# Attention scores as pairs of 64-row products instead of a block diagonal of keys, in a fused two-layer transformer kernel

## The reference, cut to what matters

```python
x = L0_attn_x                                  # (8, 512, 128)
xn = _layernorm(x, axis=-1)
k = _layernorm((xn @ Wk).reshape(b, t, 16, 8), kln_w, kln_b)
q = _layernorm((xn @ Wq).reshape(b, t, 16, 8), qln_w, qln_b)
v = (xn @ Wv).reshape(b, t, 16, 8)
dot = einsum('bqhs,bkhs->bhqk', q, k) / sqrt(8)
dot = where(causal, dot, -inf)
attn = softmax(dot, axis=-1)
out = einsum('bhqk,bkhs->bqhs', attn, v).reshape(b, t, 128) @ Wo + bo
```

## Time and profile before

| | before |
|---|---|
| median of 3 runs | 1091.5 us (1090.92 to 1092.26) |
| profiled execution, first to last instruction | 1086.1 us |
| difference, which lies outside the profiled span | 5.4 us |
| attention stage (first q unit to last pv item) | 243.1 to 629 us of the span |
| PE, ACT, DVE, POOL busy over the whole span | 919.8, 625.7, 712.3, 569.8 us |

### The profile page before, as it was taken

The page is one execution under the profiler, slowest core; times in us unless marked ns, Lnnn a source line. Parts: engine busy times, 40 slices in busy tenths (PEclk is TensorE's granted clock), DMA queues, the critical chain, the costliest instruction groups (busy, mean ns, idle before and its releaser), DMA issues.

```text
span 1086.1 us, 20632 instructions
## 1 busy us (share of the span) xinstructions
PE 919.8 (85%) x6577; PEld 615.8 (57%) x6614; DVE 712.3 (66%) x1512; ACT 625.7 (58%) x1129; POOL 569.8 (52%) x645
## 2 busy tenths in 40 slices
PE   7688879988999899899999868677788886999980
PEld 4366654477555555555555446454555655998870
DVE  6788852125777677677766565999857673646374
ACT  6466664421887687678778746344478664333320
POOL 3400019261675566656642217999306771888772
PEclk9899989999999999999999969879989998999995
DMA  5011111434010010100101049900011102223277
GB/s 144 1 78 78 77 79 58 135 128 135 21 31 21 22 30 21 31 21 21 30 21 30 2 79 149 298 11 0 1 39 43 51 28 79 83 78 92 73 204 219
DMA packets 83841, 74.46 MB, mean 69 GB/s; under 512 B 6786, under 2 KB 76876, under 8 KB 81712
## 3 DMA queue, kind: packets, MB, share of 16 engines
q1 hardware_dynamic: 73392, 64.03, 22.3%
q0 software_dynamic: 4608, 6.64, 1.9%
q10 hardware_dynamic: 5760, 2.70, 0.9%
HBM read 34.14 MB, written 33.70 MB: 62 GB/s over the span
## 4 chain that ended last, share of the span: by engine, by line
PE 32%; DVE 18%; POOL 10%; issue 9%; ACT 2%; DMA 1%; ACTq 0%; DVEq 0%; POOLq 0%
PE banks L2030 6%; PE banks L2002 5%; PE banks L2016 5%; POOL y_dram L975 4%; PE banks L2056 3%; DVE B_mneg L1150 2%; PE banks L2004 2%; DVE D_dmx L1282 2%; PE banks L2114 2%; PE banks L2069 2%; PE banks L2165 1%; DVE banks L1331 1%; DVE D_sc L1308 1%; POOL x L951 1%; DVE D_pr L1293 1%
## 5 line engine op out<-in xcount | busy, mean ns | idle before, releaser
L1150 DVE TENSOR_REDUCE B_mneg<-banks 128x2 f32<-128x256 f32 (+3 forms) x256 | 208.5, 824 | 76.9 <-PE banks L2004 68.3
L1669 ACT ACTIVATE B_pt<-banks 128x1024 f32<-128x1024 f32 (+3 forms) x256 | 178.7, 708 | 72.9 <-PE banks L2016 67.8
L792 POOL TENSOR_SCALAR_AFFINE_SELECT B_pt<-B_pt 128x512 f32<-128x512 f32 x128 | 81.2, 634 | 170.4 <-ACT B_pt L1669 161.3
L2002 PE MATMUL banks<-B_kp,B_qt 128*128 128x128 bf16 (+3 forms) x507 | 124.7, 299 | 1.8 <-DVE B_mneg L1150 0.6
L2016 PE MATMUL banks<-B_qt,B_kp 128*128 128x256 bf16 (+3 forms) x480 | 105.2, 297 | 12.1 <-issue 5.2
L2004 PE MATMUL banks<-B_mask_q,B_identb 128*128 128x128 bf16 x512 | 101.8, 219 | 0.7 <-issue 0.6
L2030 PE MATMUL banks<-B_pt,B_vp 128*32 128x512 f32 (+3 forms) x1024 | 95.5, 445 | 1.4 <-ACT B_ot L1675 0.7
L1819 ACT ACTIVATE F_gh<-banks 128x512 f32<-128x512 f32 (+1 forms) x96 | 50.0, 526 | 78.8 <-PE banks L2234 74.2
L930 POOL DMA_INDIRECT rows_dram<-F_xs,F_rowi x64 | 62.4, 975 | 60.2 <-issue 59.6
L2165 PE MATMUL banks<-D_qk 128*128 128x512 f32 x128 | 74.9, 671 | 10.2 <-DVE D_pr L1293 10.2
L975 POOL DMA_INDIRECT y_dram<-F_yo,F_ide x60 | 60.8, 1014 | 37.8 <-DVE F_yo L1510 17.4
(11 more groups left out here) (292 smaller groups left out, 2192.3 us busy)
## 6 DMA issues: line engine op xcount, KB each, us to landing
comb_dram<-C_comb SPq DMA_DIRECT2D x8, 1024.0 KB, 3.9
C_cst<-comb_dram SPq DMA_DIRECT2D x8, 1024.0 KB, 4.8
B_kp<-B_kt SPq DMA_DIRECT2D x64, 128.0 KB, 2.4
rows_dram<-D_zeros SPq DMA_DIRECT2D x8, 650.0 KB, 17.8
F_xe<-rows_dram SPq DMA_DIRECT2D x8, 650.0 KB, 3.9
C_w<-w_in SPq DMA_DIRECT2D x16, 256.0 KB, 2.9
y_dram<-D_zeros SPq DMA_DIRECT2D x2, 2048.0 KB, 19.0
F_gw<-mw_in SPq DMA_DIRECT2D x16, 256.0 KB, 3.0
```

The source lines that it names most:

```text
L792: g.affine_select(out=w, in_=w, compare_op=ALU.is_ge, fill=0.0, base=0, pattern=[[0, G], [1, P]], channel_multiplier=-1).then_inc(B_md, 1)
L1150: v.tensor_reduce(mneg[:, g % 2, qt, 2 * hp:2 * hp + 2], banks2[pair_of_banks(item)][:, :, 0:(qt + 1) * P], X, ALU.max, negate=True).then_ ...
L1669: a.activation(pt[:, 2 * hp:2 * hp + 2, PT_AT[kt]:PT_AT[kt] + w], banks2[pair_of_banks(item)][:, :, 0:w], ACT.Exp).then_inc(B_ex, 1)
L2002: t_.matmul(dst, qt1[:, g % 2, hp, qt * P:(qt + 1) * P], kp[:, g % NG, hp, h, 0:(qt + 1) * P], start=True, stop=False)
```

## The change

The block diagonal `kp`, its memset, its DMAs and the semaphores on them go away; `kt_` gets four buffers instead of two. Each product of the scores now reads only the 64 partitions of its head (`HALF[h]`), from `qt1` or `qt2` and from `kt_` directly. The mask is added by two products per head, each over 64 partitions: one for the 64 queries whose rows the head's own half of the mask holds, and one for the other 64. A new small constant, `swapped` (an identity with its halves exchanged), picks the rows; five more small POOL instructions build it and the mask's lower half. Per q unit PE issues 6 products instead of 4; per k unit 2 as before.

```diff
+HALF = (slice(0, QL), slice(QL, P))
...
-        kp = Bm("kp", [P, NG, 2, 2, T], BF16)
-        kt_ = Bm("kt", [P, 2, 2, T], BF16)
+        kt_ = Bm("kt", [P, NG, 2, T], BF16)
...
-                    for r in range(2):
-                        rows = slice(QL * r, QL * r + QL)
-                        sp.dma_start(kp[rows, g % NG, :, r, :], kt_[rows, g % 2]).then_inc(B_kp[g % NG], 16)
...
+            lower, upper = slice(0, QL), slice(QL, P)
+            own.link(g.memset(swapped[:], 0.0))
+            own.link(g.tensor_copy(mask_q[upper, lower], mask_q[upper, upper]))
+            own.link(g.memset(mask_q[upper, upper], NEG))
+            own.link(g.tensor_copy(swapped[upper, lower], identb[upper, upper]))
+            own.link(g.tensor_copy(swapped[lower, upper], identb[lower, lower]))
...
-                    if first and kind == "nb":
-                        pool.wait_ge(C_hp, NJ * EXP)
-                        g.memset(kp[:], 0.0).then_inc(B_kz, 1)
...
-                        pe.wait_ge(B_kp[g % NG], 32 * B_ROUNDS.passed(f"K{g % NG}", it, item in EARLY, "K", g, 0))
                     for h in range(2):
-                        dst = banks2[ring][:, h, 0:(qt + 1) * P]
-                        t_.matmul(dst, qt1[:, g % 2, hp, qt * P:(qt + 1) * P], kp[:, g % NG, hp, h, 0:(qt + 1) * P],
-                                  start=True, stop=False)
-                        ins = t_.matmul(banks2[ring][:, h, qt * P:(qt + 1) * P], identb[:], mask_q[:],
-                                        start=False, stop=True)
+                        t_.matmul(banks2[ring][:, h, 0:(qt + 1) * P], qt1[HALF[h], g % 2, hp, qt * P:(qt + 1) * P],
+                                  kt_[HALF[h], g % NG, hp, 0:(qt + 1) * P], start=True, stop=False)
+                    for half in range(2):
+                        for h in range(2):
+                            picks = (identb if half == h else swapped)[HALF[h], :]
+                            ins = t_.matmul(banks2[ring][:, h, qt * P + half * QL:(qt + 1) * P], picks,
+                                            mask_q[HALF[h], 0:P - half * QL], start=False, stop=(half == 1))
                     ins.then_inc(B_s1, 1)
...
-                        ins = t_.matmul(dst, kp[:, g % NG, hp, h, kt * P:(kt + 1) * P], qt2[:, g % 2, hp, kt * P:T],
-                                        start=True, stop=True)
+                        ins = t_.matmul(banks2[ring][:, h, 0:T - kt * P], kt_[HALF[h], g % NG, hp, kt * P:(kt + 1) * P],
+                                        qt2[HALF[h], g % 2, hp, kt * P:T], start=True, stop=True)
```

More of the change, by code:

```diff
@@ L181 @@
     "m": lambda x: x[0] == "m", "pv": lambda x: x[0] == "pv", "ot": lambda x: x[0] == "pv" and x[2] == NT - 1,
-    "rows": lambda x: x[0] == "q" and x[2] == 7, "misc": lambda x: x[0] in "KQZOAW",
-    "K0": lambda x: x[0] == "K" and x[1] % NG == 0, "K1": lambda x: x[0] == "K" and x[1] % NG == 1,
-    "K2": lambda x: x[0] == "K" and x[1] % NG == 2, "K3": lambda x: x[0] == "K" and x[1] % NG == 3})
+    "rows": lambda x: x[0] == "q" and x[2] == 7, "misc": lambda x: x[0] in "KQZOAW"})
 EARLY = B_ROUNDS.early
@@ L468, in build @@
         mask_q = Bm("mask_q", [P, P], BF16)
+        swapped = Bm("swapped", [P, P], BF16)
         lnw, lnb = Bm("lnw", [P, 2, D]), Bm("lnb", [P, 2, D])
@@ L482, in build @@
         aT = Bm("aT", [P, T])
-        B_in, B_const, B_kz = sem("B_ln_in"), sem("B_constants"), sem("B_kp_zero")
+        B_in, B_const = sem("B_ln_in"), sem("B_constants")
         B_ks, B_qs, B_v, B_bo = sem("B_k_split"), sem("B_q_split"), sem("B_v_padded"), sem("B_bo_added")
         B_mf, B_me = sem("B_misc_full"), sem("B_misc_empty")
-        B_kp = [sem(f"B_kp{i}") for i in range(NG)]
         B_s1, B_mx, B_m = sem("B_scores_q"), sem("B_max"), sem("B_max_in_q")
@@ L643, in _ @@
                 stage_comb(b)
[L644 to L655, removed]
-                    for r in range(2):
-                        rows = slice(QL * r, QL * r + QL)
-                        sp.dma_start(kp[rows, g % NG, :, r, :], kt_[rows, g % 2]).then_inc(B_kp[g % NG], 16)
[L659 to L666, removed]
+            for kind, b, t in FIRST_ROUND:
+                if kind == "out" and t == NT - 1 and b + 2 < B:
+                    stage_comb(b + 2)
             sp.sem_inc(B_end, 1)
@@ L1656, in turned @@
                     act.wait_ge(B_mf, B_ROUNDS.passed("misc", it, item in EARLY, kind, g, 0))
-                    if kind == "K":
-                        act.wait_ge(B_kp[(g - 2) % NG], 32 * B_ROUNDS.passed(f"K{(g - 2) % NG}", it, item in EARLY, "K", g - 2, 0))
                     a.copy(dst, bank[6][:] if kind == "A" else bank[6][:].bitcast(BF16)).then_inc(B_me, 1)
@@ L1690, in act_round @@
                     elif kind in ("K", "Q", "Z", "A"):
-                        turned(item, {"K": kt_[:, g % 2].rearrange("p a t -> p (a t)"), "Q": qt1[:, g % 2].rearrange("p a t -> p (a t)"),
+                        turned(item, {"K": kt_[:, g % NG].rearrange("p a t -> p (a t)"), "Q": qt1[:, g % 2].rearrange("p a t -> p (a t)"),
                                       "Z": qt2[:, g % 2].rearrange("p a t -> p (a t)"), "A": aT[:]}[kind])
```

1 line of the change is left out of this document (removed).

## The result

The changed kernel takes 1062.15 us (median of 4 runs, 1061.63 to 1064.18) against 1091.21 us (1088.66 to 1092.26): a ratio of 0.9741, 95% interval 0.9727 to 0.9756. It is faster by 29 us where 40 were forecast. The profiled spans are 1086.1 us before and 1059.9 us now, 26.2 apart; the remaining 3 us are in what the medians have on top of the profiled spans (5.1 us before, 2.3 now). Those 5.1 us do not all lie outside the span, as the table of the kernel before has it: every run on record takes 1.7 to 1.9 us more than its own span, and the rest is that the profiled execution of the kernel before was some 3 us faster than the median.

A forecast was written before the change was run, and what follows sets the result against it. PE was taken to set the attention stage's pace. Thirty groups saving 1.3 us each gave 39 us, plus 1 at the tail: span 1086.1 to 1046, plus 5.4 for the median, 1051 us; range 1036 to 1078.

The forecast's parts named there:

- Scores on half the array: Attention q and k units: two heads of a pair run side by side, saving 2.2 us of PE per group.
- Changes of tile shape: PE in the attention: 7.6 more shape changes per group at 0.1 us each cost 0.76 us per group.
- What lies on the path: Regular attention group: PE's part falls from 7.2 to 5.8 us, DVE's 3.45 us stay, giving 9.25 us.
- 5.8 + 3.45 + 0.1 = 9.35: Regular group in us: PE's part, DVE's part and an allowance for a nearly full ACT, instead of 10.65.
- Who is late next: Attention group: ACT is almost full, its waits for k scores shrink to little; 0.1 us added per group.
- The long intervals: Attention intervals at round ends and output projections: their extra 5.3 and 2.3 us stay, the group saving applies there too.
- The clock: Attention stage after the change: granted clock expected at 1.00, with PE busy about 8.5 of 9.35 us.
- the band of 1044 to 1060: Whole-kernel times in us in which the forecast holds, for 9.1 to 9.6 us per group: 60%.
- First round and tail: Before 275.9 us some 3.4 us saved and 2.7 lost; behind 616 us, 1 us saved by the last units.
- DMA, memset, constants: Removed 128 KB DMAs, removed 6.92 us memset and five new small POOL instructions: all hidden, priced at nothing.
- The tiles one after the other: Rival for the score products: no overlap within a pair, +0.75 us per group, 1118 us in all; chance 9%.
- The next limit binds earlier: Rival: ACT or POOL's masks hold the attention group at 9.7 to 10.2 us, 1064 to 1078 in all; chance 24%.

The follow-up runs named there:

- mask and k-unit runs: Two edits of the changed kernel: mask added by full 128-row products, ratio 0.9885; k-unit products over all 128 rows, 1092.52 us, ratio 1.0011.
- old products: Changed kernel with score products over all 128 partitions and one full mask product per head, as in the kernel before: 1168.82 us, ratio 0.9995.
- shorter POOL: Query and key norm scale and shift on 8 of 128 columns only: on the changed kernel 1134.36 us, on the kernel before 1089.2 us.

## Why the prediction was right or wrong

**Scores on half the array: right.** I took nearly all of the overlap. PE's timeline of the changed kernel, around one q unit of 512 columns between a k unit and a pv item:

```profile
387.08 0.38 PE L1995 MATMUL banks<-B_qt,B_kt 64*128 64x512 bf16 x2
387.39 0.39 PE L1979 MATMUL banks<-B_kt,B_qt 64*128 64x512 bf16 x2
387.62 0.22 PE L1984 MATMUL banks<-B_mask_q,B_identb 64*128 64x128 bf16 x1
387.62 0.24 PE L1984 MATMUL banks<-B_mask_q,B_swapped 64*128 64x128 bf16 x2
387.68 0.19 PE L1984 MATMUL banks<-B_mask_q,B_identb 64*128 64x64 bf16 x1
387.80 0.64 PE L2009 MATMUL banks<-B_pt,B_vp 128*32 128x256 f32 x8
388.37 0.34 PE L1995 MATMUL banks<-B_qt,B_kt 64*128 64x384 bf16 x2
```

Both products of a pair start within 4 ns, the first mask product 0.23 us behind them, the small one 0.06 behind that, with 0.03 of its own: 0.31 for the unit, where 0.29 and a little for the starts were forecast. The estimate that I drew from the Trainium skill's figure for four row tiles ("TensorE: Matmul & The Clock Gate", Part 3), some 1.5 times for a pair, was wrong: a pair takes the time of one of its products.

**Changes of tile shape: right.** The last mask product (387.68, 64 columns, 0.03 us) is followed after 0.12 by the pv item, so the change costs 0.09; at other places I read 0.09 to 0.11. The Trainium skill's rule that a change of tiling mode drains the engine ("TensorEngine Tiling (Array Packing)", Key Properties) agrees with the trace, between 64 and 128 rows as between 128 and 32 columns. The mask and k-unit runs confirm its price from outside.

**What lies on the path: right in its sum, with some luck.** 5.8 + 3.45 + 0.1 = 9.35 was forecast; measured are 214.3 / 23 = 9.32. But the forecast began from a group of 10.65 us, and the 23 regular intervals average 10.52: the saving is 1.21 and not 1.3. The split was less good. Of the group from one Z turn (383.32) to the next (392.75), 6.18 us lie ahead of the last maximum and 3.25 behind it. In the first part stand a pv item that begins with POOL's mask (384.42, 0.19 us late) and a q unit that waits for an exponential (385.92, 0.23 late), and one more start 0.10 late: 0.5 us of waits where I had added 0.1 for ACT. In the second part PE ends last now and not DVE, which idles before item O's division:

```profile
392.06 0.26 DVE L1146 RECIPROCAL B_orc<-banks 128x16 f32<-128x16 f32 x1 [0.43 <-PE banks L2048]
```

**Who is late next: half right.** ACT is not the bound: it is busy 69.4 of 84.2 us. But its wait for k scores fell by 9 us and not by more than half, as I had said it would. POOL, which I had priced only in a rival, is late at some masks, by 0.55 us in the interval with W, and this costs time nearly only in the long intervals.

**The long intervals: wrong, and this is the step that failed.** "The extra 5.3 and 2.3 us of the long intervals come from chains through ACT, PE and DVE at items A and W and from the branch; the change leaves them." With that I gave each of 30 intervals the full 1.3 us. The extra is not a constant on top of a PE-bound group. In an interval with W the second half belongs to DVE, 7.9 us in a row before the change. In the front, changes of shape eat what the pairs save, and POOL's late mask adds 0.6 us under the change. The four stayed at 51.6 us where I had 46.4. Five kernels with very different costs on PE all lie near that: 51.6 before, 51.7 with old products, 51.8 with the full mask, 52.2 with full k units and 51.6 with the change, and with the order of work unchanged only less of DVE's or POOL's work shortened them. At the round ends 46.4 became 47.5 where I had 42.5. Of these 5.0 us, 2.6 are the granted clock at one of them (17.92 against 15.31). The two at 1.00 did gain, 0.40 and 0.54 us against before, where I had 1.3 each. By the run with the shorter POOL some 1.9 are POOL's norm steps, 0.6 in each. The rest of 0.5 I can't assign.

**The clock: wrong in places.** I had expected 1.00 in the stage. It holds in the regular groups but for the first. Behind PE's stand at a round's end it mostly does not (3 of 4 places in the two executions of the change), and at the stage's start it does not in every execution. The first regular interval, 10.51 instead of 9.38, is 1.1 us of this kind.

**The account.** Expected 39 us in the stage, measured 26.7 (340.1 less 313.4). The difference of 12.3 is 5.2 around W, 5.0 at the round ends, and 2.1 in the regular ones, of which 1.1 is that first interval. The medians differ from the forecast by less, 1062 against 1051, and part of that is luck: I added 5.4 us on top of the span, and 2.3 were there. 1062 lies 2 us above the band of 1044 to 1060 to which I gave 60%.

**First round and tail: right, but for the stages behind.** Ahead of the stage 1.2 us were saved, 1 was forecast for both ends. Behind the last cast it takes 1.7 us more (471.8 against 470.1). The four executions on the faster chip have 474.3, 468.4, 475.4 and 468.1 us there for the change, the change without statistics, the full k units and the kernel before with the shorter POOL, so it scatters by more than that, and I assign it to nothing.

**DMA, memset, constants: right.** All at nothing, by the run with the old products.

**The rivals.** The tiles one after the other: excluded by the starts. The next limit binds earlier: its time, 1064 to 1078, nearly holds the result, but its mechanism, a regular group of 9.7 to 10.2 us, does not occur. Another engine binds in the long intervals: DVE and POOL in the four around W, POOL for 1.9 of the 5.0 us that are missing at the round ends.

## What to carry to other kernels

A gain per repetition counts only in those repetitions where the improved engine ends last, so look at each kind of interval by itself, and at the timeline of the other engines in it. The chain of waits of the kernel before went through PE up to 327 us in the interval with W; DVE's timeline showed one gap of 0.18 us from 323.5 us to the interval's end, so that a faster PE could not help in that stretch. Where row tiles of different shape alternate, price the changes (0.1 us each here) before the columns: of 242 us the pairs brought 2 with the k units left on full tiles, 13 with the mask left on them, and 28 with all in one shape.

## What the hardware showed that was not expected

**Products of different row halves start out of the order of the program.** In the run with one head after the other the second head's product started 3 to 18 ns behind the first one's in all 256 q units, ahead of two mask products that stand before it in the program. The Trainium skill ("TensorE: Matmul & The Clock Gate", Part 3) says that matmuls keep the program's order in start and end; these records show otherwise for the starts, and the measurement decides. A partner for a pair need therefore not be the next instruction.

**A small DVE instruction takes 1.05 us instead of 0.23 beside POOL.** The subtraction of the row maxima, of 128x16 elements, took over 0.4 us at 8 of its 32 places before and at 8 under the change. Timelines of the changed kernel, DVE and POOL:

```profile
400.27 1.07 DVE L1140 TENSOR_TENSOR B_qs<-B_mneg,B_qs 128x16 bf16<-128x16 f32 x1
```

```profile
400.08 1.17 POOL L808 TENSOR_TENSOR B_n<-B_n,B_qs 128x512 f32<-128x512 f32 x1
```

It ends (401.34) some 0.1 us behind POOL's instruction (401.25), and so do all eight under the change, behind a POOL instruction that had begun before them. With the shorter POOL steps one such place of 32 is left. The writing of the row maxima (line 1139) does the same: it takes over 0.4 us at 9 of 32 places under the change, 0.57 instead of 0.21 (326.29 above is one), and ends 0.06 to 0.07 behind POOL's; with the shorter POOL these are still 9. That DVE waits there for something that POOL holds is the reading; no run tried it by itself.
